# Four graph layers on 3125 nodes: strips of 16 nodes with 400 fp32 keys, block scalars merged into fewer operations, and the bias added to all input rows at once

## What is computed

```python
# layer 0: attention over the edges
score = einsum('ehd,ehd->eh', Q[dst], K[src]) / sqrt(32) + relu(efeat @ W1 + b1) @ W2 + b2
alpha = softmax of score over the edges of one destination          # 8 heads
h0 = layernorm(x + segment_sum(alpha * V[src], dst) @ Wo + bo)
# layer 1: two hops with weighted, degree-normalised sums
for _ in range(2):
    h = 0.5 * segment_sum(norm * h[src], dst) + 0.5 * h0
h1 = layernorm(h0 + relu(h) @ W.T + b)
# layer 2: weighted mean of the neighbours
h2 = layernorm(h1 + concat(segment_sum(h1[src] * w, dst) / deg, h1) @ W.T + b)
# layer 3: three unweighted hops
result = h2 @ W + b
for i in range(3):
    h = segment_sum((h * norm)[src], dst) * norm
    result += h @ W + b
out = layernorm(h2 + relu(result))
```

## Time and profile before

| | us |
|---|---|
| median of 3 runs | 3339.93 (3326.34 to 3346.44) |
| the profiled execution | 3330.41 |
| its span, first to last instruction | 3328.6 |
| QKV stage and start | 0 to 145 |
| value pass and last blocks | 145 to 878 |
| GCN1 / GCN2 / SAGE | 878 to 1404 / 1418 to 2007 / 2038 to 2592 |
| rest of layer 2, then the hops of layer 3 | 2592 to 2645, then to 3329 |

### The profile page before, as it was taken

One profiled execution on the slowest core, in us unless ns is written; L12 is line 12 of the kernel. 1 busy time (PEld: TensorE's weight loads), 2 busy tenths in 40 slices (PEclk: granted clock), 3 DMA queues, 4 the chain that ended last, 5 costly groups with the idle time before them and its releaser, 6 DMA issues.

```text
span 3328.6 us, 64436 instructions
## 1 busy us (share of the span) xinstructions
PE 2517.7 (76%) x18326; PEld 1946.3 (58%) x18430; DVE 1968.7 (59%) x6179; ACT 685.5 (21%) x1593; POOL 1739.7 (52%) x1779
## 2 busy tenths in 40 slices
PE   7688888887556555567667675777777799999997
PEld 6344444444355555555555554666566488888875
DVE  3498988888655555466666666676777511111222
ACT  3244444444100000101111111111111311111110
POOL 0476555553377777677777775777777100000000
PEclk9899999999587878778888887898888799999998
DMA  5898777774133333333333332333333123322221
GB/s 188 247 267 243 218 211 213 216 214 133 53 108 110 110 109 110 99 106 114 117 118 106 116 117 79 121 117 117 121 114 120 65 99 104 103 98 91 92 91 62
DMA packets 185642, 435.94 MB, mean 131 GB/s; under 512 B 42868, under 2 KB 89322, under 8 KB 185578
## 3 DMA queue, kind: packets, MB, share of 16 engines
q0 software_dynamic: 93184, 272.74, 28.3%
q1 hardware_dynamic: 88794, 159.17, 14.8%
q10 hardware_dynamic: 3600, 3.28, 0.3%
HBM read 390.51 MB, written 44.51 MB: 131 GB/s over the span
## 4 chain that ended last, share of the span: by engine, by line
PE 32%; POOL 25%; issue 20%; DVE 12%; DMA 6%; DVEq 1%; ACT 1%; SPq 1%; POOLq 0%; ACTq 0%
POOL gath L769 25%; PE banks L1417 17%; PE banks L1260 4%; DMA gath<-h_table,idx_slot 3%; PE banks L1307 2%; PE banks L1243 2%; DVE prod L1758 2%; PE banks L1318 1%; PE banks L1083 1%; PE banks L1195 1%; DVE rh L1762 1%; PE banks L1319 1%; DVE rh L1786 1%; PE banks L1246 1%; DMA misc<-counts 1%
## 5 line engine op out<-in xcount | busy, mean ns | idle before, releaser
L769 POOL DMA_INDIRECT gath<-h_table,idx_slot x1248 | 1285.0, 1030 | 371.2 <-issue 342.3
L1260 PE MATMUL banks<-onehot,gath 128*128 128x128 f32 x4992 | 776.2, 322 | 458.1 <-DMA gath<-h_table,idx_slot 429.9
L1260 PEld LDWEIGHTS banks<-onehot,gath 128*128 128x128 f32 x4992 | 725.7, 231 | 515.9 <-DMA gath<-h_table,idx_slot 424.4
L1417 PE MATMUL banks<-gath,misc 128*128 128x256 bf16 x1875 | 515.6, 275 | 0.0
L1417 PE MATMUL banks<-acc,misc 128*128 128x256 bf16 x2500 | 419.7, 276 | 21.3 <-DMA misc<-counts 12.0
L1318 PE MATMUL banks<-gath 128*128 128x512 bf16 x624 | 251.5, 426 | 75.0 <-DVE gath L1964 74.8
L1417 PEld LDWEIGHTS banks<-acc,misc 128*128 128x128 bf16 x2500 | 242.5, 98 | 68.5 <-issue 16.1
L767 POOL DMA_INDIRECT rh<-kv_table,idx_slot x208 | 218.5, 1050 | 121.9 <-PE banks L1234 66.5
L767 POOL DMA_INDIRECT gath<-kv_table,idx_slot x208 | 211.0, 1014 | 124.0 <-PE banks L1234 68.5
L1964 DVE TENSOR_SCALAR gath<-w_qkv 128x800 bf16<-128x800 f16 x728 | 257.3, 422 | 0.0
L1844 DVE TENSOR_TENSOR acc<-acc,banks 128x256 f32 x156 | 65.0, 417 | 324.3 <-PE banks L1260 323.9
(11 more groups left out here) (218 smaller groups left out, 3421.6 us busy)
## 6 DMA issues: line engine op xcount, KB each, us to landing
misc<-counts SPq DMA_DIRECT2D x75, 800.0 KB, 4.3
counts<-misc SPq DMA_DIRECT2D x26, 800.0 KB
gath<-h_table,idx_slot POOLq DMA_INDIRECT x1248
rh<-in_dst_rows SPq DMA_DIRECT2D x106, 128.0 KB
w_qkv<-in_ef_t SPq DMA_DIRECT2D x106, 128.0 KB
q_win<-q_table SPq DMA_DIRECT2D x210, 64.0 KB
rh<-mask_dram SPq DMA_DIRECT2D x424, 8.0 KB
kv_table<-onehot SPq DMA_DIRECT2D x25, 256.0 KB, 2.0
```

The source lines that it names most:

```text
L769: pool.indirect_dma_start(row_slot[:, k, t, :], None, source, row_index).then_inc(gath_done[k][t // HALF], 16)
L1260: last = nc.tensor.matmul(banks[:, 3 * k + c, 0:P], row_slot[:, k, t, c * P:(c + 1) * P], onehot[:, k, t, :], start=(t == 0), stop=(t == T ...
L1417: last = nc.tensor.matmul(banks[:, slot, 0:D], c_slot[:, slot, c, :], parts[n % 2][j][:, c, :], start=(c == 0 and j == 0), stop=(c == NB - ...
```

## The change

It has three parts.

1. *Strips.* A strip of 32 nodes is done as two halves of 16 (`KW`), each with a first tile of its own and 4 tiles (`ST`), 8 tiles together instead of 7. A key is now the source's block number times 16 plus the place: there are 400 columns instead of 800. They are held in fp32 instead of f16. `tile0_i` has 256 entries, and a table `strip_no` the numbers of the half strips. A half strip goes into a bank of its own: PE does eight matmuls of 400 columns.
2. *Block scalars.* The ten scalars of a block are added to one row of offsets and clipped by one row of floors; one reciprocal of nine columns serves the denominators and the count. In `norm_apply` one reciprocal serves both square roots. HDINV, HD2, HD2P and RDEG are computed once for all blocks behind the pass, and ACT waits for this (`scales_done`) before GCN1.
3. *Input rows.* `x_rows` is loaded block by block inside the QKV loop, behind each block's stores, and the bias is added to all 25 blocks by one DVE operation of 6400 columns ahead of the value pass. `bias_step` does nothing for the value pass any more, and `norm_stats` adds the input rows straight to the sums.

The core of the diff:

```diff
-ST = 7
+KW = SW // 2
+ST = 4
-SC = NB * SW
+SC = NB * KW
...
-        key_iota = w_qkv_t[:, 2 * NT:2 * NT + SC // 2].bitcast(F16)
+        key_iota = w_qkv_t[:, 2 * NT:2 * NT + SC]
...
+            def load_x(b):
+                sp.dma_start(x_rows[:, bass.ds(b, 1), :].rearrange("p a f -> p (a f)"), a["x"][bass.ds(b * P, P), :]).then_inc(b2_loaded, 16)
...
                 store_qkv(i * 2 + 1, 1)
+                load_x(i * 2)
                 free_qkv(0, i)
...
-            sp.dma_start(x_rows[:, :, :], a["x"].rearrange("(b p) f -> p b f", p=P)).then_inc(b2_loaded, 16)
...
-                    for t in range(ST):
-                        nc.tensor.matmul(banks[:, 2, :], oh_src[:, t, :], oh_key[:, t, 0:512], start=(t == 0), stop=(t == ST - 1))
-                        last = nc.tensor.matmul(banks[:, 5, 0:SC - 512], oh_src[:, t, :], oh_key[:, t, 512:SC],
-                                                start=(t == 0), stop=(t == ST - 1))
+                    for j, bank in enumerate(STRIP_BANKS):
+                        for t in range(ST):
+                            last = nc.tensor.matmul(banks[:, bank, 0:SC], oh_src[:, j * ST + t, :], oh_key[:, j * ST + t, :],
+                                                    start=(t == 0), stop=(t == ST - 1))
...
-                        link(V.tensor_copy(blk_sc[:, 0:XW], banks[:, B_ROWS, DEN_ROWS:DEN_ROWS + XW]))
-                        V.tensor_scalar(blk_sc[:, 10:11], blk_sc[:, 9:10], 1.0, None, ALU.add)
-                        V.tensor_scalar(blk_sc[:, 8:9], blk_sc[:, 8:9], 1.0, None, ALU.max)
-                        link(V.tensor_scalar(blk_sc[:, 0:HEADS], blk_sc[:, 0:HEADS], 1e-30, None, ALU.max))
-                        V.tensor_scalar(blk_sc[:, 11:12], blk_sc[:, 10:11], 0.0, None, ALU.is_gt)
-                        V.tensor_scalar(blk_sc[:, 16:17], blk_sc[:, 10:11], 1e-12, None, ALU.max).then_inc(deg_done, 1)
-                        V.reciprocal(per_node(RDEG), blk_sc[:, 8:9])
-                        link(V.reciprocal(blk_sc[:, 0:HEADS], blk_sc[:, 0:HEADS]))
+                        link(V.tensor_tensor(blk_sc[:, 0:XW], banks[:, B_ROWS, DEN_ROWS:DEN_ROWS + XW], den_offset[:, :], ALU.add))
+                        V.tensor_scalar(in_use[:, :], blk_sc[:, XW - 1:XW], 0.0, None, ALU.is_gt)
+                        V.tensor_tensor(blk_sc[:, XW:2 * XW], blk_sc[:, 0:XW], den_floor[:, :], ALU.max).then_inc(deg_done, 1)
+                        dve.wait_ge(deg_done, b + 1)
+                        rec_b = rec[:, bass.ds(b, 1), :].rearrange("p a h -> p (a h)")
+                        link(V.reciprocal(rec_b, blk_sc[:, XW:2 * XW - 1]))
...
-                    if q == PASS_VALUE:
-                        link(V.tensor_tensor(pre_b[:, :], x_b, bias[:, 0, :], ALU.add))
...
-                        V.reciprocal(blk_sc[:, 12:13], dstd[:, :])
-                    link(V.reciprocal(rstd[:, :], std[:, :]))
...
+                        link(V.reciprocal(rec2[:, :], roots2[:, :]))
+                        link(V.tensor_tensor(per_node(DINV), rec2[:, 0:1], in_use[:, :], ALU.mult))
...
-                        link(V.tensor_scalar(per_node(HDINV), per_node(DINV), 0.5, None, ALU.mult))
-                        link(V.tensor_tensor(per_node(HD2), per_node(HDINV), per_node(DINV), ALU.mult))
-                        V.tensor_scalar(per_node(HD2P), per_node(HD2), 0.5, None, ALU.add).then_inc(blk_done, 1)
+                        dve.sem_inc(blk_done, 1)
...
-                    for t in range(ST):
+                    for t in range(2 * ST):
                         last = V.tensor_scalar(oh_key[:, t, :], key_iota, key_tile[:, k, t:t + 1], None, ALU.is_equal)
...
-                dve.wait_ge(b2_loaded, 32)
+                dve.wait_ge(b2_loaded, 16 * NB + 16)
+                link(V.tensor_tensor(x_rows[:, :, :], x_rows[:, :, :], bias[:, 0, :].unsqueeze(1).to_broadcast([P, NB, D]), ALU.add))
                 make_oht(0)
...
+                V.tensor_copy(node[:, RDEG, :], rec[:, :, HEADS])
+                link(V.tensor_scalar(node[:, HDINV, :], node[:, DINV, :], 0.5, None, ALU.mult))
+                link(V.tensor_tensor(node[:, HD2, :], node[:, HDINV, :], node[:, DINV, :], ALU.mult))
+                V.tensor_scalar(node[:, HD2P, :], node[:, HD2, :], 0.5, None, ALU.add).then_inc(scales_done, 1)
```

More of the change, by code:

```diff
@@ L516, in _ @@
             free_qkv((NB - 1) % 2, (NB - 1) // 2)
+            for b in range(NB - 3, NB):
+                load_x(b)
             sp.dma_start(q_table[NP:NA, :], qkv_out[:, (NB - 1) % 2, 0:D]).then_inc(qkv_stored[(NB - 1) % 2], 16)
@@ L1091, in _ @@
             pe.wait_ge(setup_done, 1)
-            nc.tensor.transpose(banks[0:1, 7, 0:P], part_f[:, :], ident[:, :])
-            nc.tensor.transpose(banks[0:1, 7, P:2 * P], broken[:, 0:1], ident[:, :]).then_inc(pe_small, 1)
+            for c in range(2):
+                nc.tensor.transpose(banks[0:1, 7, c * P:(c + 1) * P], first_tile[:, c:c + 1], ident[:, :])
+            nc.tensor.transpose(banks[0:1, 7, 2 * P:3 * P], broken[:, 0:1], ident[:, :]).then_inc(pe_small, 1)
             def any_order_path():
@@ L1917, in norm_stats @@
                     else:
-                        link(V.tensor_tensor(ysum[:, :], ps, pre_b[:, :], ALU.add))
+                        link(V.tensor_tensor(ysum[:, :], ps, row(x_rows, b) if q == PASS_VALUE else pre_b[:, :], ALU.add))
                     link(V.bn_stats(stats[:, :], ysum[:, :]))
@@ L1977, in fused @@
                     if blocks and k % 2 == 0:
-                        chain.enter(b * size + (chain_at + 4 - size) if before else chain_at)
+                        chain.enter(b * size + (chain_at + 2 - size) if before else chain_at)
                     if full:
@@ L1987, in fused @@
                         bias_step(PASS_VALUE, b)
-                        assert chain.leave() == (size if before else 4)
+                        assert chain.leave() == (size if before else 2)
                     if value:
@@ L2007, in windows_path @@
                 add_chunk(CHUNKS - 1)
[L2008 removed]
+                chain.enter(chain_at + (NG // 2 - LAG) * size + (2 - size))
                 norm_stats(PASS_VALUE, NG // 2 - LAG - 1)
```

105 lines of the change are left out of this document (64 added, 41 removed).

## The result

The changed kernel takes 3257.3 us (median of 4, 3249.0 to 3259.2) against 3343.2 for the kernel before, measured with it: ratio 0.973, interval 0.971 to 0.976. Two later comparisons of the same pair gave 0.980 (0.977 to 0.983) and 0.982 (0.976 to 0.988). So the change saves 64 to 86 us, 1.8% to 2.7%, where 22 us under the median (0.7%) had been forecast. The time lies in the range, the size was far too small.

What follows compares the result with a forecast made beforehand. It took DVE to bound the value pass and POOL's gathers the SAGE pass. Input rows -3, value pass -30, blocks after its loop -1, strips +17 and PE 0 made -17 us: 3318 us, 8-in-10 range 3230 to 3370.

Steps and rivals of the forecast that it cites:

- The value pass: Block scalars in the value pass: fewer small DVE operations there were to save 30 us.
- I count that share: -30 us: Value pass: of 33 us less DVE work, the 0.9 share that DVE is busy was counted as time saved.
- The third rival: Value pass gives nothing because PE is late as soon as DVE is early: about 3346 us, chance 0.18.
- The start: Input rows and bias before the value pass: net -3 us, between -9 and +10.
- The strips on POOL: GCN2 and SAGE: longer runs of DVE comparisons hold POOL's gathers longer, +17 us.
- with as many stops as now: GCN2 and SAGE: stopped gathers stay at 50, each longer by 0.34 us, giving +17 us.
- The 50 stops: GCN2 and SAGE: 89 us of gather excess over GCN1, at 1.79 us a stop, read as 50 stopped gathers.
- The first rival: Stops of gathers in GCN2 and SAGE grow rarer or vanish: 3276 us with 30 stops, 3212 without any; chance 0.22.
- PE in the strip: GCN2 and SAGE: PE's matmul work falls by 231 us, costed at 0 in time.
- since POOL hides it: GCN2 and SAGE: PE's shorter strip work costed at 0 because POOL's gathers set the time.

Runs made afterwards that it cites:

- warm_before: The kernel before with six unused identity transposes on PE in the value loop, every second group, filling PE's pause ahead of L1208: ratio 0.992 (0.989 to 0.995).
- scalars_only: The kernel before with the block scalars alone merged; each block's bias addition and the one big input-row load stay: ratio 0.994 (0.992 to 0.997).
- bias_only: The kernel before with input rows loaded block by block and the bias added to all at once, scalars as before: ratio 0.997 (0.994 to 1.000).
- strips_only: The kernel before with the strips alone changed; scalars, bias and loads as before: ratio 0.994 (0.991 to 0.996).
- key_tt: The changed kernel with the key comparison as a tensor_tensor of two SBUF inputs instead of a tensor_scalar: 3436.9 us, ratio 1.036 to the kernel before.

## Why the prediction was wrong in size

*The value pass (-30 forecast, about -53 measured).* The step that failed is "I count that share: -30 us". It took the price of an operation from DVE alone, with 0.9 as the upper end of what could be had. DVE's 1.5 us a block were right, but PE's clock followed: a pause of 1.68 us behind `norm_apply` became 1.08, the low-clock stretch behind it went, and with it about a microsecond a block in which DVE had waited for the q rows. `warm_before` shows what the held clock alone is worth, 1.2 us. That the shorter pause is what held it remains argued, since in `scalars_only` the clock falls behind pauses just as short. The forecast had read PE's clock of 0.94 in the earlier trace rows and made nothing of it; the row with 1.97 us for an operation that elsewhere takes 1.13 was there to be found. The third rival, that PE would take the saving back, happened for one part: `bias_only`.

*The start (-3; measured 0 by the twelfth scores).* The first scores came 2 us earlier, and the groups behind them waited 2 us longer for their k/v rows.

*The strips on POOL (+17; measured -29 in the profile, -22 and -27 in times).* The step that failed is "with as many stops as now". A comparison, the run and the new length of a stop (2.13 us) were forecast to a few hundredths of a microsecond. But the stop had been 2.03 us already, not 1.79, so it grew by 0.1 us and not by 0.34. The 50 stops were too many as well: 39 gathers carried 79 of the 89 us. And their number fell: 32 to 47, 36 on average, in the seven profiles with the old strip and PE's old work, 22 to 33, 28 on average, in the four with the new one. The two ranges meet, so one pair of profiles can't tell the forms apart; that the strips gain is shown by the times of `strips_only` (0.991 to 0.996). The first rival named rarer stops with 0.22, at 30 stops.

*PE in the strip (0).* The step that failed is "since POOL hides it". In the new strip POOL doesn't hide PE's old work: giving it back cost 37 us, by POOL's waits for PE. In the old strip taking PE's work away didn't gain anything either: it cost 32 us. So PE's saving can't be priced apart from DVE's new comparisons, as the forecast did.

*What stays open.* Which runs stop a gather, and why the new strip stops fewer, isn't settled. Key width isn't it (f16 keys: 29), PE's shorter work alone isn't it (62). The length of the run orders nothing between 2 and 3 us (2.03 us: 29; 2.47: 32 to 47; 2.8: 22 to 33), though the longest runs, of 3.96 us in `key_tt`, had 60. With equal distances between the gather's start and the run's, some gathers were held and some passed.

## What to carry to other kernels

Where PE waits behind a busy DVE, look at what the next matmuls cost: if the same line takes two different times, an operation less on DVE can be worth more than its own time, or nothing, by what it does to PE's clock; a few idle matmuls in the pause tell what the clock is worth. Where POOL's gathers bound a pass, make DVE's long back-to-back runs short; taking them apart ended the long stops but gave nothing by itself here. The price of such a run is the held gather, and its count is to be measured over several executions, not carried over from one profile. Two engines' slack is priced together: work taken from one is free or dear depending on what is added to the other.

## What the runs showed of the hardware

The granted clock was 0.53 in the stretch behind a pause of 1.68 us (with one of 1.12 us shortly before it). It did not fall behind one of 1.08 us in the changed kernel, but in `scalars_only` it fell behind 9 of 15 pauses of 0.97 or 1.10 us. A gather beside a run of operations without gaps can be held until 0.12 or 0.82 us behind the run's end, for tensor_scalar in both widths and for tensor_tensor with two SBUF inputs (up to 4.95 us). The same comparisons in tensor_scalar form, with a short one between every two, held a gather for about half a microsecond at most (1.47 us for 0.95).
